# State-space loop: every fourth output product on VectorE, with the C row read from PSUM; the other three stay on GpSimd

## The reference, cut to what matters

```
BC = u @ W_bc + b_bc
Bcoeff, Ccoeff = jnp.split(BC, 2, axis=-1)              # 16 states each
A = -jnp.exp(A_log)                                     # (128 channels, 16 states)
dt = softplus((u @ W_dt + b_dt) @ W_dtp + b_dtp)
h[l, d, n] = exp(A[d, n] * dt[l, d]) * h[l-1, d, n] + Bcoeff[l, n] * x[l, d] * dt[l, d]
y[l, d]    = sum over n of Ccoeff[l, n] * h[l, d, n]
return y + x * Dcoeff
```

## Time and profile before

| what | value |
|---|---|
| median of 3 runs | 2200.87 us (2197.51 to 2203.46) |
| the profiled execution | 2198.03 us, its span 2196.3 us |
| PE busy | 1872.8 us (85% of the span) |
| DVE busy | 1437.4 us (65%) |
| ACT busy | 1331.5 us (61%) |
| POOL busy | 534.0 us (24%) |
| the state-space loop | from the first `inputs` at 1554.0 us to the last product's end at 1693.4 us |

### The profile page before, as it was taken

How to read it: one execution, slowest core, us unless ns; L and a number is a source line. 1 busy time by engine, 2 the same in 40 slices (tenths; PEclk the granted TensorE clock), 3 DMA queues, 4 the chain that set the end, 5 groups by cost and what they waited for, 6 DMA issues and landing times.

```text
span 2196.3 us, 23770 instructions
## 1 busy us (share of the span) xinstructions
PE 1872.8 (85%) x8324; PEld 1055.0 (48%) x8324; DVE 1437.4 (65%) x2318; ACT 1331.5 (61%) x2118; POOL 534.0 (24%) x525
## 2 busy tenths in 40 slices
PE   8999999999999989997677778997577677777998
PEld 6886444344434437884233324783122223332786
DVE  6886564456445647886755554876998755652787
ACT  6997555555555558996365555555544545566554
POOL 1443000000000002444211122222699401113221
PEclk9999999999999999998888998998899769999899
DMA  3221000000000002220000000200000000000110
GB/s 97 82 68 54 1 17 17 0 17 17 17 0 17 10 10 74 68 73 29 1 1 1 1 1 1 83 25 0 10 4 30 1 0 1 1 1 1 51 57 19
DMA packets 23746, 52.39 MB, mean 24 GB/s; under 512 B 2336, under 2 KB 6816, under 8 KB 23648
## 3 DMA queue, kind: packets, MB, share of 16 engines
q1 hardware_dynamic: 23648, 51.12, 7.3%
HBM read 49.47 MB, written 1.64 MB: 23 GB/s over the span
## 4 chain that ended last, share of the span: by engine, by line
PE 56%; DVE 22%; ACT 15%; issue 4%; POOL 1%; DMA 1%; ACTq 0%; POOLq 0%; SPq 0%; DVEq 0%
PE ps L440 9%; PE ps L442 8%; PE ps L441 8%; PE ps L708 5%; DVE arena L1439 5%; DVE arena L1184 4%; PE ps L225 4%; PE ps L701 4%; PE ps L927 3%; ACT arena L1047 2%; PE ps L897 2%; ACT rstd L242 2%; ACT arena L997 2%; ACT rstd L238 2%; PE ps L886 2%
## 5 line engine op out<-in xcount | busy, mean ns | idle before, releaser
L548 DVE TENSOR_TENSOR hid_lo<-arena,hid_hi 128x512 fp32r<-128x512 f32 x384 | 342.7, 905 | 66.5 <-ACT arena L498 64.4
L1184 DVE TENSOR_REDUCE arena<-ps 128x1 f32<-128x512 f32 (+3 forms) x352 | 213.3, 639 | 87.3 <-PE ps L901 84.1
L526 POOL TENSOR_TENSOR w_lo<-wslot,w_hi 128x512 fp32r<-128x512 f32 x56 | 76.7, 1373 | 761.4 <-DVE w_hi L543 761.4
L1104 POOL TENSOR_SCALAR_AFFINE_SELECT arena<-arena 128x256 f32<-128x256 f32 x256 | 102.9, 408 | 459.7 <-ACT arena L1047 457.1
L440 PE MATMUL ps<-x_hi,w_hi 128*128 128x512 f32 x512 | 206.4, 403 | 0.3 <-DVE arena L630 0.3
L441 PE MATMUL ps<-x_lo,w_hi 128*128 128x512 f32 x512 | 204.0, 399 | 0.0
L442 PE MATMUL ps<-x_hi,w_lo 128*128 128x512 f32 x512 | 203.8, 398 | 0.0
L495 ACT ACTIVATE hid_hi<-ps,wslot 128x512 fp32r<-128x512 f32 x256 | 177.4, 693 | 32.2 <-PE ps L442 4.6
L1047 ACT ACTIVATE arena<-ps 128x1024 f32<-128x1024 f32 (+3 forms) x256 | 166.3, 705 | 47.6 <-PE ps L917 46.9
L897 PE MATMUL ps<-arena 128*128 128x512 bf16 (+3 forms) x512 | 134.4, 328 | 65.4 <-DVE arena L1184 36.4
L498 ACT ACTIVATE arena<-ps,wslot 128x512 f32<-128x512 f32 x256 | 175.1, 684 | 0.0
(11 more groups left out here) (223 smaller groups left out, 3857.1 us busy)
## 6 DMA issues: line engine op xcount, KB each, us to landing
arena<-gates_dram SPq DMA_DIRECT2D x96, 256.0 KB, 3.5
wslot<-pack_a SPq DMA_DIRECT2D x16, 514.5 KB, 3.6
wslot<-pack_b SPq DMA_DIRECT2D x8, 901.5 KB, 4.5
wslot<-pack_c SPq DMA_DIRECT2D x8, 768.0 KB, 4.4
res<-x_in SPq DMA_DIRECT2D x4, 256.0 KB, 5.0
out_dram<-res SPq DMA_DIRECT2D x4, 256.0 KB, 2.8
bc_dram<-arena SPq DMA_DIRECT2D x1, 384.0 KB, 3.2
arena<-bc_dram SPq DMA_DIRECT2D x16, 24.0 KB
```

Of the source, the lines that this page charges most:

```text
L548: dve.tensor_tensor(hid_lo[item % 2][:, k, :], hid32[:, k, :], hid_hi[item % 2][:, k, :].bitcast(F32), ALU.subtract).then_inc(S["hid_ok"], 1)
L1184: dve.tensor_reduce(neg_max[:, i, heads[0]:heads[-1] + 1:step], ps[:, bank, 0:len(heads) * keys].rearrange("p (m k) -> p m k", k=keys), AX ...
```

## The change

Of every four rounds the last (u % 4 == 3, `on_dve`) has its output product on DVE, which reads the C row directly from PSUM bank 2 + u % 2. No copy by ACT and no product by POOL is made for these rounds. A new semaphore `ch_dve` counts DVE's products; `ch_ok` and `cc_ok` now count the other three of each four, and `upto(u)` turns a round into the two counts. DVE issues the product `outputs(u)` two iterations after its inputs: iteration v is now `inputs(v)`, then `outputs(v-2)` where that round is DVE's, then `states(v-1)`. PE waits for `ch_dve` in place of `ch_ok` in `sums` of such a round, and in `c_row(u)` where round u-2 was DVE's.

```diff
--- before.py
+++ after.py
@@ -177,7 +177,7 @@
             s2_mm exp_ok pv_mm pvs_ok t_mm t_free rden_ok pad_ok conv_ok tap_now tap_mid tap_left tap_right
             u_ok bc_mm bc_ok bc_part1 bc_rest
             bc_part2 bc_split t1_mm t1_ok z_mm z_act soft_exp soft_u soft_d soft_log soft_s dt_ok dtx_ok
-            a_exp a_ok diag_ok rows_clear bb_mm b_free cb_mm cc_ok da_ok scan_ok
+            a_exp a_ok diag_ok rows_clear bb_mm b_free cb_mm cc_ok ch_dve da_ok scan_ok
             ch_ok sum_mm tr_out cp_out""".split()
         names += [f"gate_in{s}{t}" for s in range(2) for t in range(NB)]
         S = {n: ctx.enter_context(nc.semaphore(n)) for n in names}
@@ -1291,6 +1291,13 @@
                 dve.scalar_tensor_tensor(out=res[:, t, 0:SEQ - 1], in0=ha[:, t, 1:SEQ], scalar=w[:, 2:3],
                                          in1=res[:, t, 0:SEQ - 1], op0=ALU.mult, op1=ALU.add).then_inc(S["tap_right"], 1)
 
+        def on_dve(u):
+            return u % 4 == 3
+
+        def upto(u):
+
+            return u + 1 - (u + 1) // 4, (u + 1) // 4
+
         def pe_ssm(pe, c):
             for t in range(NB):
                 pe.wait_ge(S["u_ok"], t + 1)
@@ -1307,6 +1314,12 @@
             pe.wait_ge(S["z_act"], 4)
 
             ROUNDS = NB * NSTATE
+
+            def multiplied(u):
+                if on_dve(u):
+                    pe.wait_ge(S["ch_dve"], upto(u)[1])
+                else:
+                    pe.wait_ge(S["ch_ok"], upto(u)[0])
 
             def b_row(u):
                 s, t = ITEMS[u % 8]
@@ -1319,14 +1332,16 @@
 
             def c_row(u):
                 s, t = ITEMS[u % 8]
-                if u >= 2:
-                    pe.wait_ge(S["cc_ok"], u - 1)
+                if u >= 2 and on_dve(u - 2):
+                    multiplied(u - 2)
+                elif u >= 2:
+                    pe.wait_ge(S["cc_ok"], upto(u - 2)[0])
                 pe.matmul(ps[:, 2 + u % 2, :], ones16[:, :], bc_row[:, s, 1, t, :], start=True,
                           stop=True).then_inc(S["cb_mm"], 1)
 
             def sums(u):
                 s, t = ITEMS[u % 8]
-                pe.wait_ge(S["ch_ok"], u + 1)
+                multiplied(u)
                 pe.matmul(ps[:, 4 + t, :], ident, ch[:, s, t, :], start=False, stop=False,
                           skip_group_check=True).then_inc(S["sum_mm"], 1)
 
@@ -1375,16 +1390,18 @@
                 act.activation(da[:, s], dt_s[:, :, :], ACT.Exp, scale=rate).then_inc(S["da_ok"], 1)
 
             def c_copy(u):
+                copies = upto(u)[0]
                 act.wait_ge(S["cb_mm"], u + 1)
-                if u >= 2:
-                    act.wait_ge(S["ch_ok"], u - 1)
-                act.activation(c_s[:, u % 2, :], ps[:, 2 + u % 2, :], ACT.Copy).then_inc(S["cc_ok"], 1)
+                if copies > 2:
+                    act.wait_ge(S["ch_ok"], copies - 2)
+                act.activation(c_s[:, copies % 2, :], ps[:, 2 + u % 2, :], ACT.Copy).then_inc(S["cc_ok"], 1)
 
             for s in range(2):
                 decay(0, s)
             for u in range(NB * NSTATE):
                 n, j = 2 * (u // 8), u % 8
-                c_copy(u)
+                if not on_dve(u):
+                    c_copy(u)
                 if j == 1 and n:
                     act.wait_ge(S["scan_ok"], 4 * n)
                     decay(n // 2, 1)
@@ -1434,26 +1451,39 @@
                 if t == 0:
                     dve.wait_ge(S["da_ok"], u // NB + 1)
                 dve.wait_ge(S["b_free"], u + 1)
-                if u >= 8:
-                    dve.wait_ge(S["ch_ok"], u - 7)
+                if u >= 8 and not on_dve(u):
+                    dve.wait_ge(S["ch_ok"], upto(u - 8)[0])
                 dve.tensor_tensor_scan(hst[:, s, t, :], da[:, s, t, :], db[:, s, t, :], 0.0, ALU.mult,
                                        ALU.add).then_inc(S["scan_ok"], 1)
 
-            for u in range(NB * NSTATE + 1):
+            def outputs(u):
+                s, t = ITEMS[u % 8]
+                dve.wait_ge(S["cb_mm"], u + 1)
+                dve.wait_ge(S["scan_ok"], u + 1)
+                if u >= 8:
+                    dve.wait_ge(S["sum_mm"], u - 7)
+                dve.tensor_tensor(ch[:, s, t, :], hst[:, s, t, :], ps[:, 2 + u % 2, :],
+                                  ALU.mult).then_inc(S["ch_dve"], 1)
+
+            for u in range(NB * NSTATE + 2):
                 if u < NB * NSTATE:
                     inputs(u)
-                if u:
+                if u >= 2 and on_dve(u - 2):
+                    outputs(u - 2)
+                if 1 <= u <= NB * NSTATE:
                     states(u - 1)
 
         def pool_ssm(pool, c):
             pool.memset(bc_row.rearrange("p s w t q -> p (s w t q)"), 0.0).then_inc(S["rows_clear"], 1)
             for u in range(NB * NSTATE):
+                if on_dve(u):
+                    continue
                 s, t = ITEMS[u % 8]
-                pool.wait_ge(S["cc_ok"], u + 1)
+                pool.wait_ge(S["cc_ok"], upto(u)[0])
                 pool.wait_ge(S["scan_ok"], u + 1)
                 if u >= 8:
                     pool.wait_ge(S["sum_mm"], u - 7)
-                pool.tensor_tensor(ch[:, s, t, :], hst[:, s, t, :], c_s[:, u % 2, :], ALU.mult).then_inc(S["ch_ok"], 1)
+                pool.tensor_tensor(ch[:, s, t, :], hst[:, s, t, :], c_s[:, upto(u)[0] % 2, :], ALU.mult).then_inc(S["ch_ok"], 1)
 
         def sp_ssm(sp, c):
             sp.wait_ge(S["bc_split"], 4)
```

## The result

Four executions of the changed kernel beside four of the kernel before: 2225.58 us against 2199.19, ratio 1.0105 (95% interval 1.0081 to 1.0129), so slower, by 26 us where 14 were forecast (2215 against 2200.87). It was run twice more in the experiments: 2218.82 against 2204.33 (1.0068, 1.0045 to 1.0090, 8 runs) and 2220.47 against 2202.65 (1.0072, 1.0045 to 1.0098, 6 runs), that is 14 to 18 us slower.

The account below looks back on a forecast made before the run. The loop was taken as bound by a relay of DVE's scans and POOL's products, which exclude each other. +15.8 us over the loop less 1.25 at its end, net +14.5, made 2198.03 into 2212.5, or 2215 against the median; range 2203 to 2222.

Parts of the forecast that it names:

- Relay, not load: In the loop DVE's scan and POOL's product exclude each other and alternate: scan 1.14 us, POOL 1.01, round 2.145.
- Which gap stays empty: Between scans, POOL catches up and has no product in the gap behind DVE's product, which would have hidden one whole.
- long gap: Gap after scans 3, 7, 11, ..., where DVE does inputs and its own product: 0.58 + 0.60 = 1.18 us.
- Wake-up: In short gaps a product POOL is woken for frees the scan at 1.305 us, against 1.01 queued; cycle +1.075.
- R: The moment a scan hands over, when the next DVE record starts; the scan's own record ends 0.07 to 0.08 later.
- R62: Hand-over of scan 62, at 1688.90 us in the kernel before; the loop was to lose 15.8 us.
- The end: After scan 62, the last scan goes first and the last two products run side by side: 4.95 us, saving 1.25.
- New waits at no cost: C rows waiting for DVE's products delay nothing: the copied row is ready with 2.3 us of slack before POOL wants it.
- B: Rival: in the loop POOL's wake-up costs nothing beyond a queued product; +1.4 us, 2202; chance 0.06.
- C: Rival: scans keep their 0.43 us wait in every gap and DVE's 0.60 is simply added; +8, 2209; chance 0.05.
- D: Rival: POOL's load was the loop's bound, DVE alone sets the pace afterwards; -18 us, 2183; chance 0.03.
- A: Rival: DVE asks for the scan before POOL wakes, so POOL stays a round behind; -5 us, 2196; chance 0.10.

Follow-up runs that it names:

- Experiment 1: Changed kernel with one added wait: POOL takes up round u's product only after DVE's inputs of round u+2; 2198.19 us, ratio 0.9970 to the kernel before.
- 2: Changed kernel with POOL waiting for DVE's inputs of round u+2 and every second product (32 of 64) on DVE; 2194.95 us, 0.9963 of the kernel before.
- 3: Changed kernel with every second product on DVE instead of every fourth, without the added wait on POOL; 2216.75 us, ratio 1.0058 to the kernel before.
- 5: Changed kernel with only round 3's product on DVE and the other 63 on POOL; 2216.70 us, ratio 1.0066 to the kernel before.
- experiment 4: Changed kernel with the products of rounds u % 4 == 3 and their sums left out altogether; ratio 1.0028 to the kernel before.

## Why the prediction was right in its mechanism and wrong in its time

- **Relay, not load: shown.** Experiment 1 changes only when POOL starts, 2 against 3 likewise, and 5 moves one product of 64; they move the loop by 20 to 24 us, the wait down and the moved product up. The trace of the changed kernel has the exclusion itself: a scan asked for 0.36 us after POOL's product had begun took 2.00 us (1578.03), against 1.21 where POOL had nothing to do (1644.67). DVE's product with its C row in PSUM (L1465) is outside it, with 0.67 us beside a product of POOL (1575.72 in the cycle above) as with POOL idle (1644.07). Which part of the hardware they exclude each other over, no run shows.
- **Which gap stays empty: right.** POOL catches up behind the first long gap and leaves the later ones unused: in the one from 1643.49 to 1644.67 it had been idle since 1642.49, and it started again at 1646.01.
- **Wake-up: the term a little small.** I took POOL's start 0.155 us behind R from an instruction with one wait; in the loop it is 0.22. The short round is 2.49 and not 2.445, the cycle 9.76 and not 9.655. To R62 the loop lost 17.4 us (15.8 forecast). That lies inside the bound that I had given, up to 0.15 more each time. Whether the two more waits are the reason was not tested; with the wait of experiment 2 POOL starts 0.24 us after the recorded end of `inputs` (1603.41 to 1603.65).
- **The end: the saving a little small as well.** From R62 to the addition to `x` 4.3 us (1719.10 to 1723.43) against 4.95 forecast and 6.2 before; it gave back 1.9 and not 1.25. What I mis-sized is the last four matmuls, put at 2.6: they took 1.99 here, at a granted clock of 1.00. In the third profile the same four took 2.83, at 0.68, and the end 5.2, so the term depends on the execution. In the first profile the two errors, 1.6 too little lost and 0.6 too little given back, partly cancel: 15.5 us measured, 14.5 forecast. That they come so close is in part luck.
- **New waits at no cost: right.** PE's C rows wait for DVE (37.6 us of PE's idle time) and ACT's copies wait for the C rows (82.6 us of ACT's), but POOL does not: the copy that comes after DVE's product ends 2.7 us before POOL takes it up (1645.82 and 1648.51), where 2.3 was forecast.
- **The step that failed** is the last of the sum: "So the profiled execution, 2198.03, becomes 2212.5 ... against that the forecast is 2215", with a range of 2203 to 2222. It puts everything outside the loop at no change, and the range is made of the bounds of the wake-up alone, without a term for how far executions of one program differ. The measured median, 2225.58, was outside it. The runs show what was missing: executions of the changed kernel spread over 16.6 us (2211.1 to 2227.7), while its loop stays at 156.6 to 157.5. The rest lies ahead of the loop (it begins at 1556.9 to 1566.8, with PE's granted clock at 0.89 to 0.77 in the attention stage) and behind it (501.7 to 507.9 us, at 0.88 to 0.89). The first comparison drew 11 us on top of the loop's 15.5; the other two, with more runs, drew -1 and +2, and their medians, 2218.82 and 2220.47, lie inside the range. Why the first four executions lay together at the upper end stays open.
- **Rivals.** B, C and D would have left other scans than 1.98, 1.98, 1.98 and 1.21. A did not occur by itself: POOL starts 0.36 us before DVE asks (1577.67, 1578.03).

## What to carry to other kernels

Here two engines that excluded each other both looked busy to the full while they waited for each other: POOL's products were recorded at 2165 ns before, against 1.26 to 1.28 us unhindered, and DVE's scans at 1639 ns against 1.21 us. So before taking work from one such engine, compare the durations of both with those that they have alone, and then ask in which order they will meet afterwards. The engine that had caught up paid its wake-up in every turn (a scan of 1.98 us), while the one kept a turn behind had it hidden (1.64 or 1.21), so less work cost time (6 us in experiment 4), and so did a wait removed (23.6 us of the loop in experiment 3), and a wait added saved it (20.4 in experiment 1). And where a change is worth less than one per cent, give the range the spread of the whole program and not of three runs.

## What the runs showed of the hardware that I had not expected

- One product moved out of 64 costs 19.6 us in the loop, more than the change itself (15.5): the order, once lost, did not come back in the 60 rounds that followed.
- A queued product of POOL is recorded from the end of the one before or from its wake-up, so that its waiting counts as busy: 1.97 us in experiment 2, 2.18 before, against 1.26 to 1.28 where it is not hindered. An unhindered one agrees with the scan's wait: recorded at 1.28 from 1577.67, it let the scan that was asked for at 1578.03 go 0.78 us later, at 1578.81, 1.14 after its own start.
- POOL's wake-up by a scan, with two other waits around it, takes 0.14 us from the scan's recorded end (1577.53 to 1577.67), against 0.08 with one wait.
